# A graph-attention kernel: the second chunk of rows worked in passes of 1024 rows and two heads, adjacency turned at one block in 3.0 steps

## What is computed

```python
mask = (A + jnp.eye(n)) > 0
Wh = (H @ W.T).reshape(n, HEADS, D_K)
score_l = jnp.einsum('nhd,hd->nh', Wh, a_l)
score_r = jnp.einsum('nhd,hd->nh', Wh, a_r)
e = score_l[:, :, None] + score_r.T[None, :, :]
e = jnp.where(e >= 0, e, NEG_SLOPE * e)
e = jnp.where(mask[:, None, :], e, -jnp.inf)
alpha = jax.nn.softmax(e, axis=2)
out = jnp.einsum('nhm,mhd->nhd', alpha, Wh).reshape(n, OUT_DIM)
x = _layernorm(x + jax.nn.elu(out), axis=-1)
```

## Time and profile before

| | us |
|---|---|
| median of 3 runs | 1782.24 |
| lowest and highest of them | 1779.88, 1790.67 |
| the profiled execution, its own time | 1779.54 |
| span of the profile, first to last instruction | 1777.8 |

### The profile page before, as it was taken

One profiled execution on the slowest core, in us unless ns is written; L12 is line 12 of the kernel. 1 busy time (PEld: TensorE's weight loads), 2 busy tenths in 40 slices (PEclk: granted clock), 3 DMA queues, 4 the chain that ended last, 5 costly groups with the idle time before them and its releaser, 6 DMA issues. The chain is left out here.

```text
span 1777.8 us, 80971 instructions
## 1 busy us (share of the span) xinstructions
PE 1647.8 (93%) x37067; PEld 1626.5 (91%) x37067; DVE 1685.2 (95%) x1905; ACT 1667.8 (94%) x1246; POOL 26.2 (1%) x36
## 2 busy tenths in 40 slices
PE   6788898999999999999999999999999999999995
PEld 6788798899999999999999999999999998999995
DVE  6999999998979989999999999999899999999997
ACT  4999999989899999999999999999999999999992
POOL 0000000000001000000000100000000100000000
PEclk9899999999999999999999999999999999999998
DMA  8996888999998876675766676676667131121111
GB/s 278 344 346 206 277 293 266 341 313 328 310 307 293 257 246 198 205 243 182 244 202 223 207 242 215 209 235 208 224 189 236 35 82 58 37 58 37 35 37 37
DMA packets 241476, 368.10 MB, mean 207 GB/s; under 512 B 12912, under 2 KB 103408, under 8 KB 239600
## 3 DMA queue, kind: packets, MB, share of 16 engines
q1 hardware_dynamic: 241136, 362.92, 62.9%
HBM read 345.57 MB, written 17.30 MB: 204 GB/s over the span
## 5 line engine op out<-in xcount | busy, mean ns | idle before, releaser
L505 ACT ACTIVATE bmask<-lrow,rtab 128x2048 fp8e4<-128x2048 f32 (+1 forms) x975 | 1547.9, 1666 | 49.8 <-PE psum L414 47.5
L414 PE MATMUL psum<-vring,cmask 128*128 128x99 bf16 x14336 | 716.4, 208 | 30.5 <-DVE cmask L730 26.5
L414 PE MATMUL psum<-vring,bmask 128*128 128x99 bf16 x14336 | 722.0, 208 | 19.2 <-issue 15.6
L414 PEld LDWEIGHTS psum<-vring,cmask 128*128 128x128 fp8e4 x14336 | 662.0, 98 | 42.5 <-DVE cmask L730 35.8
L414 PEld LDWEIGHTS psum<-vring,bmask 128*128 128x128 fp8e4 x14336 | 667.4, 97 | 21.3 <-issue 17.5
L730 DVE SCALAR_TENSOR_TENSOR cmask<-acache,bmask 128x1024 int32<-128x1024 int32 x512 | 623.5, 1218 | 19.8 <-PE psum L414 19.5
L725 DVE SCALAR_TENSOR_TENSOR bmask<-acache,bmask 128x1024 int32<-128x1024 int32 x512 | 624.1, 1219 | 8.4 <-ACT bmask L505 4.6
L706 DVE TENSOR_SCALAR bmask<-lrow,rtab 128x2048 fp8e4<-128x2048 f32 (+1 forms) x305 | 316.8, 1052 | 0.0
L383 PE MATMUL trp<-pack,abuf 128*128 128x64 bf16 x4096 | 143.9, 194 | 32.3 <-ACT acache L474 23.5
L383 PEld LDWEIGHTS trp<-pack,abuf 128*128 128x128 bf16 x4096 | 132.6, 99 | 35.2 <-issue 35.0
L414 PE MATMUL psum<-vt,bmask 128*128 128x99 bf16 x2048 | 107.1, 211 | 12.2 <-issue 9.7
(11 more groups left out here) (64 smaller groups left out, 264.1 us busy)
## 6 DMA issues: line engine op xcount, KB each, us to landing
abuf<-in_adj_dram SPq DMA_DIRECT2D x256, 1024.0 KB, 8.4
vring<-v_scratch SPq DMA_DIRECT2D x384, 99.0 KB, 2.9
lrow<-l_scratch SPq DMA_DIRECT2D x16, 1024.0 KB, 7.9
v_scratch<-vt SPq DMA_DIRECT2D x16, 792.0 KB, 11.2
vring<-v_scratch SPq DMA_DIRECT2D x64, 198.0 KB, 6.0
cmask<-in_x_dram SPq DMA_DIRECT2D x16, 256.0 KB, 5.0
late<-in_x_dram SPq DMA_DIRECT2D x16, 256.0 KB, 5.2
out_dram<-late SPq DMA_DIRECT2D x16, 256.0 KB, 3.6
```

The source lines that it names most:

```text
L414: return nc.tensor.matmul(psum[:, bank, at * S3:(at + 1) * S3], mask[:, j * P:(j + 1) * P], values, start=opening, stop=True, skip_group_c ...
L505: last = nc.scalar.activation(to, rows, ACT.Relu, bias=rtab[:, 2 * s + i, H + h:H + h + 1], scale=BIG, saturate=False)
```

## The change

The second chunk is worked like the first. Passes 4 and 5 take its first half (two heads each), passes 6 and 7 its second half. So passes 4 to 7 become narrow; passes 8 to 15 stay wide. The order of the blocks follows: all of chunk 1's first half, then its second half. The blocks 16 to 95 are turned at one in 3.0 steps from step 32 to step 269, and chunk 3's last 32 blocks at one in 3.9 from step 272, as before. The layer norm of chunk 1 is done in two parts (8 rows per partition in pass 6, 8 in pass 8) in place of one part of 16 in pass 8, with a store for each, and the self loops of its second half are set in pass 5. The waits follow these places. `load_v`, `load_lrow`, `compares`, `on_vector` and `adj_words` are not edited; they go by `narrow(w)`.

```diff
--- before.py
+++ after.py
@@ -35,8 +35,9 @@
     FACTOR = [0.125 / v for v in BIT_VALUE]
 
 
-    UNITS = [[(0, half, 2 * pair + u) for u in range(2)] for half in range(2) for pair in range(2)]
-    UNITS += [[(c, u, h) for u in range(2)] for c in range(1, NC) for h in range(H)]
+    NARROW = 2
+    UNITS = [[(c, half, 2 * pair + u) for u in range(2)] for c in range(NARROW) for half in range(2) for pair in range(2)]
+    UNITS += [[(c, u, h) for u in range(2)] for c in range(NARROW, NC) for h in range(H)]
     PASSES = len(UNITS)
     JUST_MADE = 2
     Q = PASSES * STEPS
@@ -47,13 +48,14 @@
 
 
 
-    BLOCKS = [(0, half, m) for half in range(2) for m in range(QUADS)] + [(c, half, m) for c in range(1, NC) for m in range(QUADS) for half in range(2)]
+    BLOCKS = [(c, half, m) for c in range(NARROW) for half in range(2) for m in range(QUADS)]
+    BLOCKS += [(c, half, m) for c in range(NARROW, NC) for m in range(QUADS) for half in range(2)]
     NB = len(BLOCKS)
     BLOCK_NO = {b: n for n, b in enumerate(BLOCKS)}
     AHEAD = 2
     FIRST_TURNS = {0: 2, 1: 3, 2: 4, 4: 5, 6: 6, 7: 7, 9: 8, 11: 9, 13: 10, 15: 11, 17: 12, 19: 13, 21: 14, 23: 15}
 
-    LATER_TURNS = [STEPS + n * 12 // 5 for n in range(3 * QUADS)] + [148 + n * 39 // 10 for n in range(NB - 4 * QUADS)]
+    LATER_TURNS = [STEPS + n * 3 for n in range(5 * QUADS)] + [272 + n * 39 // 10 for n in range(NB - 6 * QUADS)]
 
     def turned_at(q):
 
@@ -66,7 +68,7 @@
 
     def emptied_after(n):
 
-        return 1 if n < QUADS else 2 if n < 4 * QUADS else 3
+        return 1 if n < QUADS else 2 if n < 6 * QUADS else 3
 
     EMPTIED = [[n for d in (1, 2, 3) if q >= d for n in TURNED[q - d] if emptied_after(n) == d] for q in range(Q)]
     assert [n for e in EMPTIED for n in e] == list(range(AHEAD, NB))
@@ -100,7 +102,8 @@
         ON_VECTOR.append(ON_VECTOR[q] + (on_vector(q) > 0))
 
 
-    FINISHED = [(1, range(0, SUB)), (3, range(SUB, JC))] + [(4 * c + 3, range(JC)) for c in range(1, NC - 1)]
+    FINISHED = [(4 * c + 2 * half + 1, range(half * SUB, (half + 1) * SUB)) for c in range(NARROW) for half in range(2)]
+    FINISHED += [(4 * c + 3, range(JC)) for c in range(NARROW, NC - 1)]
     FINISHED += [(PASSES - 1, range(0, SUB)), (PASSES - 1, range(SUB, JC))]
     HALVES = [slice(0, SUB), slice(SUB, JC)]
     ROWS_DONE = [sum(len(js) for _, js in FINISHED[:e]) for e in range(len(FINISHED) + 1)]
@@ -318,14 +321,14 @@
                 if w == 2 and s == 4:
                     sp.wait_ge(v_lo, JUST_MADE * NG)
                     load_xr(0, 1)
-                if w == 2 and s == 22:
-                    store_y(0, 0, ROWS_DONE[1])
+                if w in (2, 6) and s == 22:
+                    store_y(w // 4, 0, ROWS_DONE[w // 2])
                 if w % 4 == 0 and w > 0:
                     c = w // 4
                     if s == 24:
                         for half in range(2):
-                            if (c - 1, half) != (0, 0):
-                                store_y(c - 1, half, ROWS_DONE[c + 1])
+                            if c > NARROW or half == 1:
+                                store_y(c - 1, half, ROWS_DONE[min(2 * c, c + NARROW)])
                     if s == 28:
                         sp.wait_ge(y_stored, 32 * 2 * c)
                         for half in range(2):
@@ -714,7 +717,7 @@
                 if s % EVERY_STEPS == 0:
                     for c, half, _ in UNITS[w]:
                         dve.wait_ge(evac_done, BLOCK_NO[c, half, 2 * (s // EVERY_STEPS) + 1] + 1)
-                if w in (0, 2) or w % 4 == 0:
+                if w in (2, 6) or w % 4 == 0:
                     own = [(c, half, 2 * (s // EVERY_STEPS) + i) for c, half, _ in UNITS[w] for i in range(2)]
                     loops = [DIAGONALS.index(b) for b in own if b in DIAGONALS]
                     if loops:
@@ -878,11 +881,11 @@
                 if s == 0 and w > 0:
                     take_first_sums(w - 1)
                     take_last_sums(w - 1)
-                if w == 1 and s in (12, 14):
-                    add_diagonal(0, 2 + (s - 12) // 2)
+                if w in (1, 5) and s in (12, 14):
+                    add_diagonal(w // 4, 2 + (s - 12) // 2)
                 if w > 0 and w % 4 == 0:
                     c = w // 4
-                    for k in range(4):
+                    for k in range(4 if c >= NARROW else 2):
                         if s == 8 * c - 3 + k + 2 * (k // 2):
                             add_diagonal(c, k)
                 if s == 1 and w > 0:
```

## The result

The median went from 1782.70 to 1788.22 us over 20 runs each; the ratio is 1.0028 (95% interval 1.0015 to 1.004). That is slower by about 5 us, less than the 1% said to be telling in the prediction but clear of noise with this many runs of each kernel. Forecast were 1789 us and +6.5 us. Sums over passes of two profiled executions are therefore no finer than a few us; where they and the ratios of the medians disagree by so much, the ratios have many runs behind them.

What follows compares the result with a forecast made beforehand. Three engines in near balance, TensorE last, with stalls in narrow passes following the DMA load; -1.5 - 12.3 + 22.6 - 2.3 = +6.5 us on 1779.54 gives 1786.0, 1788.7 at the median, said as 1789; range 1772 to 1808.

Steps and rivals of the forecast that it cites:

- The deciding term: Passes 2 to 7: a narrow pass with turns at one in 3.0 steps takes 108.8 us, range 106.1 to 111.3.
- the two parts of the trade: Passes 2 and 3 together save 12.3 us through fewer turns; passes 4 to 7, made narrow, lose 22.6 us.
- a sign of error: Passes 4 to 7: TensorE waiting for VectorE's masks by more than 3 us a pass would make the prediction wrong.
- Rival 1: Passes 2 to 7: stalls don't fall with the turning rate; 111.3 us a pass, 1803.6 us at the median; chance 22%.
- Rival 2: Passes 2 to 7: no stalls are left, VectorE bounds at 106.1 us a pass; 1772.4 us at the median; chance 14%.
- Rival 3: Passes 2 to 7: ScalarE becomes the bound at 115 us a pass, giving 1825.8 us; chance 4%.
- The small terms: Outside the trade: 1.5 us saved in pass 1, 2.3 us in pass 8; moved layer norm, self loops and store at 0.
- The stretch up to pass 2: Pass 1: fewer turns save 1.5 us of ScalarE's copies, since ScalarE is full there.
- Pass 8: Pass 8: half the layer norm leaves ScalarE, 3.5 us, two more copies cost 1.2 us; 2.3 us saved.
- The layer norm in pass 6: Pass 6: the moved half, 3.5 us of ScalarE's work, lies in ScalarE's slack and costs nothing.

## Why the prediction was right, and where it wasn't

**The deciding term was right in size.** I took 108.8 us for a narrow pass with turns at one in 3.0 steps; the six took 651.0 us, 108.5 each (109.5 in the profile of fewer compares on VectorE, which lies at its median). With it the two parts of the trade came out: -11.6 for -12.3, +20.0 for +22.6. Reading the passes apart, and seeing that the slower turning would help two passes while four would pay for it, was what the forecast stood on.

**Its working was half right: which engine came last.** "The sides lie within 4 us of each other, with TensorE last", with 5.5 us of stalls a pass. The stalls were 2.1, 3.0, 6.2, 0.6, 2.7 and 0.2, 2.5 in the mean. TensorE was busy for 103.2 in the mean (102.5 said), waited for no copy (0.8 said), and waited 2.5 for VectorE's `cmask` (nothing said). I had named more than 3 us of this wait in passes 4 to 7 as a sign of error: pass 6 passed it with 4.0, the mean of the four, 2.2, did not. VectorE's work was as said, 104.8 in the mean (104.7 said); with 3.4 at the end (1.4 to 3.9 said) it makes 108.2 of 108.5, so VectorE was as full as TensorE, where I had put TensorE last alone. So TensorE and VectorE bind together. That also explains why relieving VectorE alone gave little: taking 5 us of its work out of each of four passes gave 5.5 us in all, moving three compares to ScalarE gave nothing. Two errors of the same size cancelled here, stalls too large by 3 us and a TensorE that would never wait for VectorE. That the sum came out within 1 us a pass is in this part luck.

**The stalls were scaled by the wrong thing.** I set them by the total GB/s and let the small packets speak for more. Doubling the value loads in wide passes did not raise them; halving the blocks' bytes took them away, in passes 2 and 3 of the kernel before and in passes 5 and 6 of the changed one. What matters most is the adjacency blocks' traffic, and in passes 2 and 3 the turning rate sets it: the four kernels that turn and load there as before had 5.3 to 6.8 us of stalls in pass 2 and 6.4 to 7.1 in pass 3, the changed kernel and the three runs of it with the same turns and loads there 1.9 to 4.3 and 1.8 to 3.4. Elsewhere no simple rule holds: the earlier turning had 2.5 us of stalls in pass 1 at 325 GB/s, where TensorE isn't last, and 6.3 in pass 4 at 263.

**The stalls are a late supply of TensorE's instructions.** I had taken this without a row for it; the traces have one. The page of the kernel before lists a DMA queue for instructions (packets, MB, share):

```profile
q8 instruction: 292, 4.78, 1.1%
```

These are packets of 16 KB, one to every 256 of the 74812 records of TensorE's two queues. In the 13 traces there are 301 issue stalls in passes 2 to 8, and every one of them ends 1.2 to 1.6 us after such a packet has landed; of moments taken at random there, 8% do.

The packets come late because they start late. To see it, count packets (from 0) and TensorE's instructions from the beginning, and write down for packet n how many instructions past 256n TensorE is when the packet starts. The mean of this lag in pass 2 is 330 in the kernel before, 297 in the changed one and 256 with half of the blocks' bytes, while the packet itself takes 1.04, 1.02 and 1.08 us. An instruction takes 23 ns there, so the blocks' full traffic puts a packet off by 1.7 us. In no trace does TensorE, from pass 0 to 10, get further than 449 past 256n before the packet has landed. In passes 4 to 7 of the changed kernel the mean lag is 309, with half of the value loads 299, with half of the blocks' bytes 238; double value loads in the wide passes add 4 to 11. So the value loads have a part, a small one. Parting the block loads did not help in passes 2 and 3 (347 and 348, 330 and 335 before) but brought the lag from 306 to 284 in pass 4, where that run gained. What a packet waits for before it starts the records don't say.

**Rival 1** (stalls stay, 111.3 a pass) didn't come: the stalls did fall with the turning rate, from 5.7 and 7.1 to 2.1 and 3.0 us in passes 2 and 3. The Trainium skill, "DMA: Bandwidth & Descriptors", section "Queues, rings and completion order", says that a DMA engine goes round its queues by packets; I had drawn from it that thinning the blocks would not shorten the stalls, and the runs show that it does (1.1 us in place of 5.7 with half of the bytes). The instruction packets do start later under the blocks' traffic, by 1.7 us; how the engines go round their queues no run here shows. **Rival 2** (no stalls) is the changed kernel with half of the blocks' bytes, 106.7 a pass; its price for VectorE's bound (106.1) was right, its condition wasn't met. **Rival 3** (ScalarE at 115) was excluded rightly: ScalarE was busy for 102 to 108 us in the narrow passes though its compares last 1148 ns each, since neighbours overlap. It has little room in a pass with a layer norm, though: 108.4 of 110.5 us in pass 2.

**The small terms.** The stretch up to pass 2 gave 4.1 us where I had counted ScalarE's copies alone (1.5). Pass 8 gave 1.4 of 2.3. The layer norm in pass 6 was priced at nothing; passes 4 and 6, which hold it, are 3.1 and 3.7 us longer than 5 and 7. Part of that is their longer stalls (6.2 and 2.7 us against 0.6 and 0.2); with half of the blocks' bytes, where next to no stalls are left, they are 2.8 and 1.0 us longer, so it isn't free. VectorE's part of it stood in the forecast, in the mean of passes 2 and 3, one of which has it.

## What to carry to other kernels

Where several engines are busy for 95% of the span, cut the trace by stage and price each engine's whole account in a stage (busy time, its waits, what it can't avoid at the end); a sum over the nearest stages gave the change to within 2 us, here with two errors of 3 us a pass cancelling in it. Spreading a background load evenly pays, but look at what must change to allow it: here the same evenness was had for less by moving turns into pass 1, where TensorE had room (0.9962 in place of 1.0028). When two engines bind together, relieving one tells little; the experiment that takes the suspected cause of its stalls away tells most. And where the profile gives a stall no name, lay its end beside the landings of every kind of DMA packet before you settle for a guess.

## What the runs showed of the hardware

TensorE stands still when its instructions come late: all 301 unnamed stalls end 1.2 to 1.6 us after a 16 KB instruction packet has landed. Large loads beside it put the start of these packets off (by 1.7 us on the average at 324 against 211 GB/s in pass 2) and not their transfer (1.04 and 1.08 us).

It depends on which traffic: 30 GB/s more of value loads (242 against 212 GB/s, in pass 5, where 8 blocks are turned) added no stall, and 100 GB/s less of adjacency blocks (201 to 211 in place of 304 to 324 GB/s in passes 2 and 3) took 7 to 9 us a pass away. Which property of the block loads does it (their size, their rows, or the time in which the DMA engines have no gap) isn't settled.
